# Attention and channel-mix layer on one core: the bf16 split of the projections, with the high part subtracted by TensorE in the PSUM bank

## The reference, cut to what matters

```python
q = (x @ Wq + bq); k = x @ Wk + bk; v = x @ Wv + bv      # q: 256 columns, k and v: 64 each
scores = einsum('bghqd,bgkd->bghqk', q, k) / sqrt(16)
mask = (i - 128)[:, None] >= j[None, :] | (i[:, None] < j[None, :])
att = softmax(where(mask, -1e9, scores)); out = att @ v
x = layernorm(x + out @ Wo + bo)
xr = mu_r * x + (1 - mu_r) * x_prev; xk = mu_k * x + (1 - mu_k) * x_prev
x = layernorm(x + sigmoid(xr @ W_r.T) * (relu(xk @ W_k.T) ** 2 @ W_v.T))
```

## Time and profile before

| what | value |
| --- | --- |
| three runs, median | 453.26 us |
| lowest and highest of them | 449.74 and 453.81 us |
| span of the profiled execution | 449.1 us |
| mean granted TensorE clock in it | 0.952 |
| VectorE busy | 344.6 us (77%), 852 instructions |
| ScalarE busy | 272.8 us (61%), 566 instructions |
| GpSimd busy | 291.2 us (65%), 466 instructions |

### The profile page before, as it was taken

The page is one execution under the profiler, slowest core; times in us unless marked ns, Lnnn a source line. Parts: engine busy times, 40 slices in busy tenths (PEclk is TensorE's granted clock), DMA queues, the critical chain, the costliest instruction groups (busy, mean ns, idle before and its releaser), DMA issues.

```text
span 449.1 us, 8432 instructions
## 1 busy us (share of the span) xinstructions
PE 407.7 (91%) x2542; PEld 251.9 (56%) x2542; DVE 344.6 (77%) x852; ACT 272.8 (61%) x566; POOL 291.2 (65%) x466
## 2 busy tenths in 40 slices
PE   8976999997999979997999979997999979999853
PEld 3444546664556656564556665564656656665532
DVE  5765775898678976899688986799878988996551
ACT  2512567775667747764677657666577657778522
POOL 4552666776487856677487766688487767876531
PEclk9986899998999989999999989999999989999995
DMA  8484585412733175321753146421823144000000
GB/s 324 115 141 91 134 148 138 100 49 46 140 101 84 50 94 146 82 66 43 110 163 86 49 74 152 87 60 47 120 65 94 49 62 70 14 13 27 12 23 23
DMA packets 50892, 39.25 MB, mean 87 GB/s; under 512 B 33696, under 2 KB 42400, under 8 KB 50720
## 3 DMA queue, kind: packets, MB, share of 16 engines
q1 hardware_dynamic: 50416, 37.93, 38.9%
q10 hardware_dynamic: 432, 0.79, 0.6%
HBM read 26.38 MB, written 12.06 MB: 86 GB/s over the span
## 4 chain that ended last, share of the span: by engine, by line
PE 64%; DVE 19%; ACT 6%; issue 6%; DMA 2%; POOL 1%; SPq 1%; ACTq 0%; DVEq 0%; POOLq 0%
PE av_ps L983 11%; PE score_ps L969 9%; PE proj_ps L893 8%; PE max_ps L952 6%; PE gen L1070 6%; PE gen L1024 6%; PE gen L1081 5%; PE gen L1059 4%; DVE neg_max L704 4%; DVE q_tiles L696 3%; DVE max_parts L711 3%; PE max_ps L943 3%; ACT parts L517 2%; DVE mix L780 2%; PE av_ps L1040 2%
## 5 line engine op out<-in xcount | busy, mean ns | idle before, releaser
L410 POOL TENSOR_SCALAR_AFFINE_SELECT probs<-probs 128x512 f32<-128x512 f32 x252 | 168.2, 678 | 108.0 <-ACT probs L535 105.7
L535 ACT ACTIVATE probs<-score_ps 128x512 f32<-128x512 f32 x252 | 148.4, 598 | 86.0 <-PE score_ps L969 85.6
L969 PE MATMUL score_ps<-qs,ks 98*128 98x512 bf16 x252 | 99.8, 398 | 2.2 <-ACT probs L535 1.4
L704 DVE TENSOR_REDUCE neg_max<-max_ps 128x3 f32<-128x480 f32 x144 | 87.4, 631 | 12.3 <-PE max_ps L952 12.1
L983 PE MATMUL av_ps<-probs,vals 128*32 128x512 f32 x504 | 67.0, 605 | 0.9 <-POOL probs L410 0.8
L969 PEld LDWEIGHTS score_ps<-qs,ks 98*128 98x128 bf16 x252 | 25.0, 100 | 57.3 <-ACT probs L535 47.9
L1070 PE MATMUL gen<-mix,rest_w 128*128 128x128 f32 x256 | 38.7, 299 | 16.9 <-DVE mix L780 15.5
L952 PE MATMUL max_ps<-ks,q_tiles 96*128 96x160 bf16 x416 | 52.3, 243 | 0.0
L417 POOL TENSOR_TENSOR rstd<-var,minus_half 128x1 f32<-128x1 f32 x64 | 35.7, 558 | 21.7 <-DVE var L728 20.8
L1070 PEld LDWEIGHTS gen<-mix,rest_w 128*128 128x128 f32 x256 | 35.4, 208 | 22.7 <-DVE mix L780 17.8
L780 DVE SCALAR_TENSOR_TENSOR mix<-diff,first,x_t 128x128 f32<-128x128 f32 x128 | 43.8, 385 | 0.0
(11 more groups left out here) (86 smaller groups left out, 663.2 us busy)
## 6 DMA issues: line engine op xcount, KB each, us to landing
qs<-q_parts SPq DMA_DIRECT2D x48, 192.0 KB, 6.1
q_parts<-parts SPq DMA_DIRECT2D x48, 128.0 KB, 2.2
x_t<-x_feat SPq DMA_DIRECT2D x8, 512.0 KB, 3.7
x_in<-x_nat SPq DMA_DIRECT2D x8, 512.0 KB, 4.5
out<-out_t SPq DMA_DIRECT2D x32, 128.0 KB, 2.0
ks<-k_parts SPq DMA_DIRECT2D x42, 80.0 KB, 2.9
qs<-q_parts SPq DMA_DIRECT2D x42, 64.0 KB, 2.2
k_parts<-parts SPq DMA_DIRECT2D x8, 192.0 KB, 2.8
```

What stands on the lines that cost most here:

```text
L410: nc.gpsimd.affine_select(out=v, in_=v, compare_op=ALU.is_ge if i % 2 else ALU.is_gt, fill=0.0, base=0, pattern=[[0, HPG], [sign, BLK]], c ...
L535: nc.scalar.activation(probs[:, buf, i], score_ps[i % 2][:, :], ACT.Exp, scale=SCALE).then_inc(s_exp, 1)
L704: nc.vector.tensor_reduce(neg_max[:, TPB * i:TPB * i + n], max_bank(t, j, i)[:, 0:n * TILE_KEYS].rearrange("p (n k) -> p n k", k=TILE_KEYS ...
L969: nc.tensor.matmul(score_ps[i % 2][:, :].rearrange("p (h q) -> p h q", q=BLK), ks[0:ROWS + MPARTS, par, g, k0:k0 + BLK], qs[0:ROWS + MPART ...
```

## The change

TensorE gets a constant, `minus_b`, the negative identity in bf16. After the high part is written, one more product of `minus_b` with the high part is added into the projection's bank (`take_high`), so that the bank then holds p - high without its bias. ScalarE makes the middle part straight out of the bank with the bias added (`middle_part`), and VectorE makes the low part out of the same bank, the bias and the middle part (`low_part`). The array `rest`, `rest_part` and GpSimd's `low_part` are gone. The bank is now free only when the low part is done, and the waits for it are on `s_lo`. Slot 1 leaves `THREE_BANKS`, since `proj_ps` holds chunk 1 during slot 0, in which the maxima of slot 1's block are made.

```diff
-THREE_BANKS = (1, 2, 3)
+THREE_BANKS = (2, 3)
...
         def _(pool):
-            def low_part(s, m):
-                pool.wait_ge(s_mid, s * NCH + m + 1)
-                nc.gpsimd.tensor_tensor(parts[:, m, 2], rest[:, m], parts[:, m, 1], ALU.subtract).then_inc(s_lo, 1)
...
         def _(act):
-            def middle_part(s, m):
-                act.wait_ge(s_rest, s * NCH + m + 1)
-                nc.scalar.copy(parts[:, m, 1], rest[:, m]).then_inc(s_mid, 1)
+            def middle_part(s, m, ps=None):
+                act.wait_ge(s_sub, s * NCH + m + 1)
+                nc.scalar.activation(parts[:, m, 1], (ps or proj_ps)[:, 0:SB], ACT.Identity,
+                                     bias=small_cols[:, m:m + 1]).then_inc(s_mid, 1)
...
         def _(dve):
-            def rest_part(s, m, ps=None):
-                dve.wait_ge(s_hi, s * NCH + m + 1)
-                if m == 0:
-                    dve.wait_ge(s_pcp, s + 1)
-                if later(s, 1):
-                    dve.wait_ge(s_lo, s * NCH - NCH + m + 1)
-                nc.vector.scalar_tensor_tensor(out=rest[:, m], in0=(ps or proj_ps)[:, 0:SB],
-                                               scalar=small_cols[:, m:m + 1], in1=parts[:, m, 0],
-                                               op0=ALU.add, op1=ALU.subtract).then_inc(s_rest, 1)
+            def low_part(s, m, ps=None):
+                dve.wait_ge(s_mid, s * NCH + m + 1)
+                nc.vector.scalar_tensor_tensor(out=parts[:, m, 2], in0=(ps or proj_ps)[:, 0:SB],
+                                               scalar=small_cols[:, m:m + 1], in1=parts[:, m, 1],
+                                               op0=ALU.add, op1=ALU.subtract).then_inc(s_lo, 1)
...
                 if maxima:
                     tile_max(t + 1, jn, 0)
                     tile_max(t + 1, jn, 1)
+                if ahead and j == 0:
+                    low_part(s + 1, 1)
                 if f4:
                     gate(t - 4)
...
-                if coming and j == 3:
-                    rest_part(s + 2, 0)
-                if ahead and j == 0:
-                    rest_part(s + 1, 2)
                 if f1:
                     normalise()
+                if coming and j == 3:
+                    low_part(s + 2, 0)
+                if ahead and j == 0:
+                    low_part(s + 1, 2)
                 if maxima and (project or j < SB_BLKS - 2):
                     tiles_ahead()
...
-                if coming and j == 3:
-                    rest_part(s + 2, 1)
...
         def _(pe):
             def project_chunk(s, m, par, ps=None):
...
                 elif ps is None:
-                    pe.wait_ge(s_rest, s * NCH + m)
+                    pe.wait_ge(s_lo, s * NCH + m)
...
+            def take_high(s, m, ps=None):
+                pe.wait_ge(s_hi, s * NCH + m + 1)
+                if m == 0:
+                    pe.wait_ge(s_pcp, s + 1)
+                nc.tensor.matmul((ps or proj_ps)[:, 0:SB], minus_b[:, :], parts[:, m, 0], start=False, stop=True,
+                                 skip_group_check=True).then_inc(s_sub, 1)
...
+                if ahead and j == 0:
+                    take_high(s + 1, 1)
                 if maxima:
                     max_scores(t + 1, jn, pn, 0, s, project)
                     max_scores(t + 1, jn, pn, 1, s, project)
...
                 if f3:
                     r_product(t - 3)
+                if coming and j == 3:
+                    take_high(s + 2, 0)
...
                 if f3:
                     k_product(t - 3)
+                if ahead and j == 0:
+                    take_high(s + 1, 2)
```

More of the change, by code:

```diff
@@ L161, in attention_channel_mix @@
         s_masks = sem("s_masks")
+        s_minus = sem("s_minus")
         s_zero = sem("s_zero")
@@ L173, in attention_channel_mix @@
         s_hi = sem("s_hi")
-        s_rest = sem("s_rest")
+        s_sub = sem("s_sub")
         s_mid = sem("s_mid")
@@ L447, in start @@
                 pool.wait_ge(s_restw, 16)
-                for m in range(NCH):
-                    low_part(0, m)
                 x_plus_bo(0, 0)
-                low_part(1, 0)
                 x_plus_bo(1, 1)
-                low_part(1, 1)
-                low_part(1, 2)
             def step(s, j, par, project, coming, maxima, scores):
@@ L492, in step @@
                     mask(t, 5, j % 2)
-                if coming and j == 3:
-                    low_part(s + 2, 0)
-                if ahead and j == 0:
-                    low_part(s + 1, 2)
                 if scores and t:
@@ L541, in start @@
                 act.wait_ge(s_first, 16)
+                first_banks, second_banks = (proj_ps, max_ps[0], max_ps[1]), (gen0, gen1, av_ps)
                 for m in range(NCH):
-                    high_part(0, m, (proj_ps, max_ps[0], max_ps[1])[m])
+                    high_part(0, m, first_banks[m])
                     if m:
-                        middle_part(0, m - 1)
-                middle_part(0, NCH - 1)
+                        middle_part(0, m - 1, first_banks[m - 1])
+                middle_part(0, NCH - 1, first_banks[NCH - 1])
                 high_part(1, 0, gen0)
                 high_part(1, 1, gen1)
-                middle_part(1, 0)
+                middle_part(1, 0, gen0)
                 high_part(1, 2, av_ps)
@@ L555, in start @@
                                   ).then_inc(s_stack0, 16)
-                middle_part(1, 1)
-                middle_part(1, 2)
+                middle_part(1, 1, second_banks[1])
+                middle_part(1, 2, second_banks[2])
             def step(s, j, par, project, coming, maxima, scores):
@@ L740, in start @@
                 nc.vector.tensor_copy(ident_b[:, :], ident[:, :]).then_inc(s_masks, 1)
+                nc.vector.tensor_scalar(minus_b[:, :], ident[:, :], -1.0, None, ALU.mult).then_inc(s_minus, 1)
                 for m in range(NCH):
-                    rest_part(0, m, (proj_ps, max_ps[0], max_ps[1])[m])
+                    low_part(0, m, (proj_ps, max_ps[0], max_ps[1])[m])
                 val_copy(0, 0)
@@ L747, in start @@
                 nc.vector.tensor_copy(first_mask[:, :, :], first_f[:, :, :]).then_inc(s_masks, 1)
-                rest_part(1, 0, gen0)
-                rest_part(1, 1, gen1)
-                rest_part(1, 2, av_ps)
+                low_part(1, 0, gen0)
+                low_part(1, 1, gen1)
+                low_part(1, 2, av_ps)
                 val_copy(1, 1)
@@ L902, in v_turn @@
                 else:
-                    pe.wait_ge(s_rest, s * NCH + (NCH if later(s, 1) else 1))
+                    pe.wait_ge(s_lo, s * NCH + (NCH if later(s, 1) else 1))
                 if later(s, 2):
@@ L999, in start @@
                     project_chunk(0, m, 0, (proj_ps, max_ps[0], max_ps[1])[m])
+                pe.wait_ge(s_minus, 1)
+                for m in range(NCH):
+                    take_high(0, m, (proj_ps, max_ps[0], max_ps[1])[m])
                 pe.wait_ge(s_ident, 1)
+                for m in range(NCH):
+                    project_chunk(1, m, 1, (gen0, gen1, av_ps)[m])
                 v_turn(0)
                 for m in range(NCH):
-                    project_chunk(1, m, 1, (gen0, gen1, av_ps)[m])
+                    take_high(1, m, (gen0, gen1, av_ps)[m])
                 v_turn(1)
```

9 lines of the change are left out of this document (3 added, 6 removed).

## The result

The changed kernel takes 489.77 us (median of 4 runs, 487.39 to 492.7) against 451.8 us (4 runs, 449.74 to 453.81): 1.082 times as long, 95% interval 1.075 to 1.090. The forecast was 490 us, with a range of 473 to 502.

What follows compares the result with a forecast made beforehand. TensorE's in-order queue was taken to set the pace. Span 449.1 us, plus 33 for six rounds of 5.5 and 3.5 for slow clock, gave 485.6; with the median 4.2 above the span, 490 us, range 473 to 502.

Steps and rivals of the forecast that it cites:

- steps 1, 2: Slot 3: TensorE waits at chunk 0's `take_high`, then chunk 1 waits for chunk 0's low part; +0.4 us each a round.
- step 3: Head of slot 0: TensorE waits 0.7 us for chunk 1's high part, then runs its product; +0.95 us a round.
- step 4: Slot 0: group 4, on two banks, waits for `tile_max` 2, queued behind chunk 1's low part; +2.8 us a round.
- step 5: End of slot 0: chunk 2's low part delays `tile_q` and so group 0 of slot 1; +1.0 us a round.
- The products: TensorE: 18 added products in the loop at 0.22 us each, 4.0 us within the rounds' sum.
- The clock: TensorE at 1.2 GHz after long waits: two more slow stretches, +3.5 us, bounds 0 and +10 us.
- Start and end: Start: low parts about as early, fillers later, first blocks wait for a DMA; 0 taken, bounds -1.5 and +2.5 us.
- Rival A: Slack in TensorE's queue covers the waits, only the products count: +4.0 us, 457 us; chance 4%.
- B: Only step 4 and the products cost, existing waits such as slot 2's 2.58 us absorb the rest: about 474 us; 13%.
- C: VectorE relieved of GpSimd's contention: 1.3 us a round, 8 us in all, giving 449 us or less; chance 4%.

Runs made afterwards that it cites:

- small_low: The kernel before with GpSimd's low part cut to one column of 512 in the loop's six rounds; 447.4 us, ratio 0.986.
- low1_late: The changed kernel with chunk 1's low part moved on VectorE behind `tile_max` 3 and the first half of the mix; 467.94 us, ratio 1.026.
- two_banks: The kernel before with slot 1's block on two banks for its row maxima instead of three; 452.87 us, ratio 0.997.
- take1_behind: The changed kernel with the product of chunk 1's high part moved on TensorE behind row-maximum group 1; 489.02 us, ratio 1.072.
- tileq_first: The changed kernel with `tile_q` moved on VectorE ahead of the low parts of chunks 0 and 2; 470.1 us, ratio 1.030.
- no_products: The kernel of all_three without the loop's 18 products that take the high part away; 452.13 us, ratio 0.994.
- fill_wait: The changed kernel with 11 products of zeros in TensorE's wait ahead of group 4 in slot 0; 485.63 us, ratio 1.070.
- all_three: The changed kernel with the moves of low1_late, take1_behind and tileq_first together; 455.18 us, ratio 1.001.

## Why the prediction was right

The mechanism came as forecast; the number met closer than the sum did. The sum was 449.1 + 33 + 3.5 = 485.6 us of span; the profiled span is 488.5. Term by term, by TensorE's starts in the earlier trace rows and the timeline above:

| stretch | before | after | more | forecast |
| --- | --- | --- | --- | --- |
| chunk 0 (before: 169.52) to chunk 1 (steps 1, 2) | 5.82 | 6.73 | 0.91 | 0.8 |
| chunk 1 to group 0 of slot 0 (step 3) | 1.94 | 2.99 | 1.05 | 0.95 |
| group 0 to group 4 (step 4) | 3.41 | 6.20 | 2.79 | 2.8 |
| group 4 to chunk 2 | 3.89 | 4.12 | 0.23 | 0 |
| chunk 2 to group 0 of slot 1 (step 5) | 5.05 | 6.03 | 0.98 | 1.0 |
| whole clean round | 50.07 | 55.76 | 5.69 | 5.5 |

The stretches sum to 5.96 us; the rest of the round gives 0.27 us back. From group 0 of slot 1 to slot 2's mix products it is 21.56 us, as in small_low (21.57), where the kernel before takes 21.86: that is what GpSimd's absence gives.

- *Step 4* is half the sum, and low1_late shows its cause: the same work, later in one queue, and the wait is gone, with the bank still missing. The bank is a condition of it, since group 4 waits for `tile_max` 2 only with two banks, as the prediction says; by itself it costs 0.63 us a round (two_banks).
- *Steps 3 and 5* are shown by the waits that vanish in take1_behind and tileq_first; in microseconds of the trace they are 0.62 and 1.2 us a round. Step 3's wait is 0.56 us and not 0.7.
- *The 0.23 us* between group 4 and chunk 2 I had put at nothing. TensorE's row-maximum group 5 waits for `tile_max` 3 there.
- *Reason wrong, number right:* step 5 explained the 1.06 us of `tile_q` by GpSimd's low part. small_low shows it unchanged with one column of the low part, beside the same masks. In the changed kernel it takes 0.68 us at 325.13, where it has moved to a time at which GpSimd is idle.
- *The products*, 0.22 us each: the timeline after has the spacing, 309.30 to 309.52, and no_products has it for the third product alone (chunk 2 to group 0, 4.58 to 4.36 us); for the other two it does not separate product and wait. The Trainium skill's 131 ns for a sustained stream (page "TensorE: Matmul & The Clock Gate", section "Back-to-back issue gap") is not what these rows show.
- *The clock:* I took two further slow stretches of 1.7 us, 3.5 us in all. It is three further ones, and they cost about 3.6 us: from the first chunk 0 of the loop to the last it is 288.90 us against 256.85, 32.05 us more, of which five rounds' waits make 28.45. The size was right because two errors met: more stretches, each cheaper at the new wait (1.2 to 1.3 us). fill_wait shows that they hang on the idleness and not on the wait as such. That they are three and not six is not explained; the runs differ in it.
- *Start and end:* the first chunk 0 of the loop comes at 66.66 instead of 65.99 us, and 0.9 us is lost behind the last round; I had 0 for both.
- *Rival A* falls (the products have no slack to hide in and the waits none either), *B* too: slot 2's wait is 2.58 us as before, so it takes up nothing. *C* is real in size but small: GpSimd's absence gives 0.3 us a round at full clock, not 1.3. The Trainium skill's rule (page "Perfetto Trace Analysis", section "Optimizing Scalar/DVE Operations") that GpSimd and VectorE share a port agrees with the second residual's 1.37 and 0.41 us and with the cast's 2.28 and 0.18 us; it says nothing on whether VectorE is what the time hangs on.

That the forecast met the median within 1 us is luck. The span was 2.9 us above the sum: 1.1 us from the rounds (34.1 for 33), 0.7 at the start, 0.9 behind the last round and 0.1 from the clock, with rounding. The 4.2 us put on top for the median were 2.9 us too many: the median of the changed kernel stands 1.3 us above the profiled span. The 4.2 came from a median of three runs, 453.26 us; with the fourth run it is 451.8.

## What to carry to other kernels

Where the bounding engine's queue has no gaps, price a change by walking each new wait through the queues behind it: which instruction sits in front of the one that releases the bound engine, and could it stand later? Three such places made most of 38 us here, and moving three calls brought the total back to that of the kernel before, though 0.9 us a round was left and a better clock covered it. When an operation on a helper engine is suspected of slowing another engine, look for the one long operation that meets the short ones on the path; cutting one 2.36 us addition into four and moving the pieces off the path was worth 4 to 5%, while taking the loop's low parts off the same engine was worth 0.3 us a round at full clock.

## What the runs showed of the hardware that I had not expected

- The slow-clock stretches make total times misleading for differences under some 5 us: all_three's ten runs lie between 452.97 and 457.92 us with clocks of 0.957 to 0.977, and the ratio 1.001 hides 0.9 us a round. A clean round repeats within 0.1 us.
- 66 products of zeros, 14 us of TensorE's work, shortened the kernel by some 4 to 6 us (ratio 1.070 against 1.082, intervals just meeting; 6.3 us between the traces), since TensorE was idle there anyway and kept its 2.4 GHz behind it.
- Two kernels whose waits of 2.58 us in slot 2 are the same have from two slow stretches in the loop (all_three) to six (small_low). What decides it is open.
